# A circuit stage's first 20 microseconds in another order: Sin's table, the scans, sixteen columns, and who splits the weights

## The reference

```python
def quantum_circuit(v):
    return jnp.cumprod(jnp.cos(v), axis=-1)
x  = x + attention(layernorm(x), ctx, ctx)
xh = layernorm(x).reshape(B, T, H, dk)                 # 16 heads of 16 columns
x1 = layer_norm(xn + quantum_circuit(xh).reshape(B, T, C), gamma1, beta1)
q  = quantum_circuit(x1[..., :16])
h  = jnp.einsum('btq,fq->btf', q, w1) + b1             # 16 -> 1024
ffn = jnp.einsum('btf,cf->btc', jax.nn.relu(h), w2) + b2
x  = x + layer_norm(x1 + ffn, gamma2, beta2)
x  = x + experts(layernorm(x))
```

## Time and profile before

| | us |
| --- | --- |
| median of 3 runs (1952.27 to 1953.28) | 1952.32 |
| the profiled execution's own time | 1960.63 |
| its span in the profile | 1958.8 |
| TensorE busy in the span | 1885.8 |
| VectorE busy | 1468.4 |
| ScalarE busy | 1134.9 |
| GpSimd busy | 650.0 |

### The profile page before, as it was taken

How to read it: one execution, slowest core, us unless ns; L and a number is a source line. 1 busy time by engine, 2 the same in 40 slices (tenths; PEclk the granted TensorE clock), 3 DMA queues, 4 the chain that set the end, 5 groups by cost and what they waited for, 6 DMA issues and landing times. The chain is left out here.

```text
span 1958.8 us, 46585 instructions
## 1 busy us (share of the span) xinstructions
PE 1885.8 (96%) x18804; PEld 1783.4 (91%) x18804; DVE 1468.4 (75%) x2800; ACT 1134.9 (58%) x1917; POOL 650.0 (33%) x636
## 2 busy tenths in 40 slices
PE   7899999999999999999999999999879889999998
PEld 5899999999999999999999999999757789999998
DVE  6777777777777777777777777777777567666667
ACT  2556655666665566666656665666656435566652
POOL 3222233322223232222323222233021135888960
PEclk9999999999999999999999999999969699999999
DMA  8666667666666666666666666667311136666633
GB/s 270 172 155 160 172 156 179 158 163 154 160 170 159 173 160 164 152 162 168 162 160 172 164 155 160 166 166 182 106 59 44 54 113 210 210 220 223 226 115 135
DMA packets 146790, 313.85 MB, mean 160 GB/s; under 512 B 57888, under 2 KB 77216, under 8 KB 143120
## 3 DMA queue, kind: packets, MB, share of 16 engines
q1 hardware_dynamic: 140672, 295.03, 55.7%
q0 software_dynamic: 4752, 13.38, 2.3%
q10 hardware_dynamic: 1152, 2.47, 0.5%
HBM read 134.20 MB, written 18.35 MB: 78 GB/s over the span
## 5 line engine op out<-in xcount | busy, mean ns | idle before, releaser
L440 ACT COPY a_pT<-a_pst 128x512 f32<-128x512 f32 x768 | 421.7, 583 | 412.8 <-PE a_pst L936 412.8
L446 ACT ACTIVATE a_probs<-a_probs,a_nmax 128x1601 f32<-128x1601 f32 x256 | 418.7, 1636 | 142.0 <-DVE a_probs L608 141.9
L608 DVE TENSOR_SCALAR_CACHE_REDUCE a_probs<-a_pss 128x1608 f32<-128x1608 f32 x256 | 467.5, 1826 | 12.4 <-PE a_pss L925 10.8
L936 PE MATMUL a_pst<-a_id,a_probs 128*128 128x128 f32 (+1 forms) x3328 | 454.9, 275 | 11.4 <-ACT a_pT L440 9.0
L936 PEld LDWEIGHTS a_pst<-a_id,a_probs 128*128 128x128 f32 (+1 forms) x3328 | 384.9, 141 | 49.6 <-issue 21.4
L353 POOL TENSOR_TENSOR a_tick<-a_tick 128x1 f32<-128x1 f32 x62 | 12.0, 193 | 951.0 <-DMA a_raw<-in_ctxT 865.2
L626 DVE TENSOR_SCALAR a_khi<-a_psk,a_bk 128x402 fp32r<-128x402 f32 x250 | 158.6, 635 | 143.5 <-PE a_psk L890 141.3
L358 POOL TENSOR_TENSOR a_clo<-a_raw,a_chi 128x402 fp32r<-128x402 f32 x240 | 247.4, 1062 | 4.8
L925 PE MATMUL a_pss<-a_kst,a_bd 96*128 96x402 f32 x1024 | 240.7, 357 | 8.0 <-DVE a_v L633 5.8
L888 PE MATMUL a_pso<-a_whi,a_chi 128*128 128x256 f32 (+1 forms) x806 | 241.3, 299 | 0.0
L890 PE MATMUL a_pso<-a_whi,a_clo 128*128 128x256 f32 (+1 forms) x806 | 226.6, 281 | 0.0
(11 more groups left out here) (248 smaller groups left out, 3511.7 us busy)
## 6 DMA issues: line engine op xcount, KB each, us to landing
a_kst<-a_khi SPq DMA_DIRECT2D x1008, 100.5 KB, 2.6
a_kst<-a_klo SPq DMA_DIRECT2D x504, 100.5 KB, 2.6
a_raw<-in_ctxT SPq DMA_DIRECT2D x60, 804.0 KB, 5.6
f_gur<-in_wgu SPq DMA_DIRECT2D x24, 1408.0 KB, 6.2
f_dr<-in_wd SPq DMA_DIRECT2D x24, 768.0 KB, 4.7
a_bd<-q_scr SPq DMA_DIRECT2D x192, 32.0 KB, 2.0
e_big<-ys_scr SPq DMA_DIRECT2D x8, 512.0 KB, 6.7
a_pT<-in_ctxT SPq DMA_DIRECT2D x2, 1608.0 KB, 8.8
```

Of the source, the lines that this page charges most:

```text
L440: nc.scalar.copy(pT[:, p % HALF, 4 * i:4 * i + 4, :], ps_t[:, i % 2, :].rearrange("p (t q) -> p t q", q=P)).then_inc(t_copied_act, 1)
L446: nc.scalar.activation(pr, pr, ACT.Exp, bias=nmax[:, b, p:p + 1], scale=-1.0, accum_out=esum[:, b, p:p + 1]).then_inc(probs_ready, 1)
L608: nc.vector.tensor_scalar(probs[:, p % 2, :].rearrange("p (b k) -> p b k", b=QK), ps_s[:, :, 0:KQ], -SCALE, None, ALU.mult, ALU.min, accum ...
L936: mm = nc.tensor.transpose(ps_t[0:r, i % 2, (t % 4) * P:(t % 4 + 1) * P], probs[:, p % 2, t * P:t * P + r], a_id_sb[:])
```

## The change

- ScalarE: Sin's table is loaded before the last three copies (`table.0`), cos.0 and cos.1 come next, then two copies, cos.2, the third copy, cos.3. The lists now hold these copies, and TensorE's holds the last transposes, the weighing and the projection, in the order as before.
- VectorE: `scan` is a stage of its own, apart from `residual`. All four lists are in a new order.
- `centre_q` scales only the first 16 columns of groups 0 and 1; `centre1` scales the other 240 of these groups later, and q_angles.0 and .1 wait for `centre_q` alone.
- GpSimd zeroes `heads` in four instructions (two of them before the keys are stacked), zeroes the first column of each head in `c` and in `qc`, which VectorE did, and splits w1, which VectorE did, ahead of its list. centre1 of the groups that lie where w1 was loaded waits for this split, and so does each first `expand` of a group.

```diff
         DVE_ORDER = order(
-            "rows.0 ends.0 residual.0 norms.0 residual.1 scale1.0 last_rows.0 scale1.1 q_angles.0 affine.0 circuit.0 q_angles.1 affine.1 circuit.1 residual.2 "
-            "residual.3 scale1.2 residual.4 scale1.3 add.0 sums.0 scale1.4 q_angles.2 scale2.0 q_angles.3 circuit.2 q_angles.4 circuit.3 circuit.4 add.1 sums.1 "
-            "round.5 reduce.5 scale2.1 second.0 affine.2 residual.5 second.1 scale1.5 add.2 scale3.0 scale3.1 affine.3 affine.4 q_angles.5 affine.5 circuit.5 add.3 "
...
+            "rows.0 scan.0 residual.0 ends.0 scan.1 scale1.0 residual.1 q_angles.0 norms.0 circuit.0 scan.2 residual.2 last_rows.0 scale1.1 scale1.2 affine.0 "
+            "q_angles.1 scan.3 circuit.1 q_angles.2 scan.4 circuit.2 residual.3 residual.4 add.0 scale1.3 sums.0 scale1.4 round.5 reduce.5 q_angles.3 q_angles.4 "
+            "scan.5 circuit.3 residual.5 scale2.0 affine.1 affine.2 circuit.4 add.1 affine.3 affine.4 add.2 scale1.5 second.0 q_angles.5 sums.1 circuit.5 scale3.0 "
+            "affine.5 add.3 sums.2 scale2.1 second.1 scale2.2 add.4 scale3.1 second.2 add.5 sums.3 scale3.2 scale2.3 second.3 add.6 sums.4 scale3.3 scale2.4 "
...
-            "cos.0 cos.1 cos.2 cos.3 cos.4 centre1.0 centre1.1 q_cos.0 angle.5 q_cos.1 copy_q.0 relu.0 relu.1 relu.2 relu.3 relu.4 relu.5 relu.6 copy_q.1 relu.7 "
-            "relu.8 relu.9 relu.10 relu.11 relu.12 relu.13 relu.14 relu.15 centre1.2 centre1.3 centre1.4 q_cos.2 centre2.0 q_cos.3 q_cos.4 copy_q.2 relu.16 relu.17 "
-            "copy_q.3 relu.18 relu.19 relu.20 relu.21 relu.22 relu.23 relu.24 relu.25 cos.5 copy_q.4 centre2.1 relu.26 relu.27 centre1.5 centre3.0 centre3.1 "
...
+            "table.0 cos.0 cos.1 copies.0 cos.2 copies_end.0 cos.3 centre_q.0 centre1.0 cos.4 q_cos.0 copy_q.0 relu.0 relu.1 relu.2 relu.3 relu.4 relu.5 relu.6 "
+            "relu.7 centre_q.1 centre1.1 centre1.2 q_cos.1 angle.5 copy_q.1 q_cos.2 relu.8 relu.9 relu.10 relu.11 copy_q.2 relu.12 relu.13 relu.14 relu.15 relu.16 "
+            "relu.17 centre1.3 centre1.4 cos.5 q_cos.3 relu.18 relu.19 relu.20 relu.21 copy_q.3 relu.22 relu.23 relu.24 relu.25 q_cos.4 centre2.0 relu.26 relu.27 "
+            "relu.28 copy_q.4 centre1.5 q_cos.5 exp_table.0 centre3.0 relu.29 relu.30 relu.31 copy_q.5 relu.32 copy_x.0 centre2.1 centre2.2 centre3.1 relu.33 "
+            "relu.34 relu.35 relu.36 relu.37 relu.38 relu.39 relu.40 centre2.3 relu.41 relu.42 centre3.2 relu.43 relu.44 relu.45 relu.46 relu.47 centre3.3 "
...
         PE_ORDER = order(
-            "turn_q.0 expand.0 expand.1 expand.2 expand.3 expand.4 expand.5 expand.6 expand.7 turn_q.1 expand.8 expand.9 expand.10 expand.11 expand.12 expand.13 "
-            "expand.14 expand.15 contract.0 contract.1 turn_q.2 expand.16 expand.17 turn_q.3 expand.18 expand.19 turn_q.4 expand.20 expand.21 expand.22 expand.23 "
-            "expand.24 expand.25 contract.2 expand.26 expand.27 contract.3 expand.28 expand.29 turn_x.0 expand.30 expand.31 turn_q.5 expand.32 turn_x.1 contract.4 "
...
+            "turn_last.0 turn_end.0 weigh.0 project.0 turn_q.0 expand.0 expand.1 expand.2 expand.3 expand.4 expand.5 expand.6 expand.7 contract.0 turn_q.1 expand.8 "
+            "expand.9 expand.10 expand.11 turn_q.2 expand.12 expand.13 expand.14 expand.15 expand.16 expand.17 contract.1 expand.18 expand.19 expand.20 expand.21 "
+            "turn_q.3 expand.22 expand.23 expand.24 expand.25 contract.2 expand.26 expand.27 turn_q.4 expand.28 contract.3 expand.29 expand.30 turn_x.0 expand.31 "
+            "turn_q.5 expand.32 contract.4 contract.5 expand.33 expand.34 expand.35 expand.36 expand.37 expand.38 expand.39 expand.40 expand.41 expand.42 "
+            "contract.6 expand.43 expand.44 expand.45 expand.46 expand.47 logits.0 contract.7 turn_x.1 turn_x.2 logits.1 turn_x.3 logits.2 turn_x.4 logits.3 "
+            "turn_x.5 turn_x.6 logits.4 logits.5 logits.6 turn_x.7 logits.7 ")
...
+        Q_FIRST = 2
+        HEADS_ZERO, C_ZERO, W1_ZERO, QHEADS_ZERO, QC_ZERO, QT_ZERO = 4, 5, 6, 7, 8, 9
...
-            sp.wait_ge(heads_zeroed, 1)
+            sp.wait_ge(zeroed, HEADS_ZERO)
...
-            for m in range(NC):
-                for z in range(PIECES):
-                    pool.wait_ge(stacked[m][z], COPIES * B)
-            nc.gpsimd.memset(heads[:], 0.0).then_inc(heads_zeroed, 1)
+            for i in range(0, NT, 4):
+                if i == NT // 2:
+
+                    for m in range(NC):
+                        for z in range(PIECES):
+                            pool.wait_ge(stacked[m][z], COPIES * B)
+                nc.gpsimd.memset(heads[:, i:i + 4, :], 0.0).then_inc(zeroed, 1)
             pool.wait_ge(s_filled, PAIRS * B)
             pool.wait_ge(o_filled, 2 * (B - 1))
-            nc.gpsimd.memset(w1_sb[:].bitcast(F32), 0.0).then_inc(heads_zeroed, 1)
-            nc.gpsimd.memset(q_heads[:], 0.0).then_inc(heads_zeroed, 1)
-            nc.gpsimd.memset(qT[:].bitcast(F32), 0.0).then_inc(heads_zeroed, 1)
+            nc.gpsimd.memset(c[:].rearrange("p t (h d) -> p (t h) d", d=HD)[:, :, 0], 0.0).then_inc(zeroed, 1)
+            nc.gpsimd.memset(w1_sb[:].bitcast(F32), 0.0).then_inc(zeroed, 1)
+            nc.gpsimd.memset(q_heads[:], 0.0).then_inc(zeroed, 1)
+            nc.gpsimd.memset(qc[:, :, 0], 0.0).then_inc(zeroed, 1)
+            nc.gpsimd.memset(qT[:].bitcast(F32), 0.0).then_inc(zeroed, 1)
+            pool.wait_ge(loaded, 16 * 7)
+            pool.wait_ge(zeroed, W1_ZERO)
+            nc.gpsimd.tensor_copy(w1_sb[0:3 * HD, :], w1_raw).then_inc(w1_split, 1)
+            pool.wait_ge(w1_split, 1)
+            nc.gpsimd.tensor_tensor(out=w1_sb[2 * HD:3 * HD, :], in0=w1_raw[2 * HD:, :], in1=w1_sb[2 * HD:3 * HD, :].bitcast(F32), op=ALU.subtract).then_inc(w1_split, 1)
+            pool.wait_ge(w1_split, 2)
...
-            g = PAIRS * B - 1
             act.wait_ge(expo_set, 1)
             act.wait_ge(kv_filled, STEPS * B)
-            for i in range(3):
-                copy_tiles(g, PAIRS - 1, i)
-            nc.scalar.activation(first_sin[:], x1_ex[:, 0:1], ACT.Sin)
 
             def centre(g, n, out, src):
 
                 act.wait_ge(scale_set[n], g + 1)
+                if n == 1 and sum(GROUPS[g]) > NT // 2:
+
+                    act.wait_ge(w1_split, 2)
+                cols = slice(HD if n == 1 and g < Q_FIRST else 0, D)
                 for i in each(g):
-                    last = nc.scalar.activation(out[:, i, :], src[:, i, :], ACT.Identity, bias=shift[:, i:i + 1], scale=rstd[:, i:i + 1])
+                    last = nc.scalar.activation(out[:, i, cols], src[:, i, cols], ACT.Identity, bias=shift[:, i:i + 1], scale=rstd[:, i:i + 1])
                 last.then_inc(centred[n], 1)
 
             for stage, g in ACT_ORDER:
                 f = lambda z: flat(z, g)
-                if stage == "angle":
+                if stage == "table":
+                    nc.scalar.activation(first_sin[:], x1_ex[:, 0:1], ACT.Sin)
+                elif stage == "copies":
+                    for i in range(2):
+                        copy_tiles(PAIRS * B - 1, PAIRS - 1, i)
+                elif stage == "copies_end":
+                    copy_tiles(PAIRS * B - 1, PAIRS - 1, 2)
+                elif stage == "centre_q":
+                    act.wait_ge(scale_set[1], g + 1)
+                    for i in each(g):
+                        last = nc.scalar.activation(a[:, i, 0:HD], t[:, i, 0:HD], ACT.Identity, bias=shift[:, i:i + 1], scale=rstd[:, i:i + 1])
+                    last.then_inc(q_centred, 1)
+                elif stage == "angle":
                     angles(units_to(g) - 1)
                 elif stage == "cos":
 
                     act.wait_ge(reduced, units_to(g))
-                    act.wait_ge(heads_zeroed, 1)
+                    act.wait_ge(zeroed, C_ZERO)
...
-                    act.wait_ge(heads_zeroed, 3)
+                    act.wait_ge(zeroed, QC_ZERO)
...
-            ch(nc.vector.memset(c[:].rearrange("p t (h d) -> p (t h) d", d=HD)[:, :, 0], 0.0))
-            ch(nc.vector.memset(qc[:, :, 0], 0.0))
 
             for stage, g in DVE_ORDER:
                 f = lambda z: flat(z, g)
@@ -829,23 +855,24 @@
                     leave_turns(units_to(g) - 1)
                 elif stage == "rows":
                     dve.wait_ge(loaded, 16 * 7)
-                    dve.wait_ge(heads_zeroed, 2)
-                    ch(nc.vector.tensor_copy(w1_sb[0:3 * HD, :], w1_raw))
                     ch(nc.vector.tensor_tensor(ffn_row[:], row[:, B1, :], row[:, FB, :], ALU.add))
                     ch(nc.vector.tensor_scalar(q_row[:, 0, :], row[:, G1, 0:HD], 1.0 / (2.0 * np.pi), None, ALU.mult))
                     ch(nc.vector.tensor_scalar(q_row[:, 1, :], row[:, B1, 0:HD], 1.0 / (2.0 * np.pi), 0.25, ALU.mult, ALU.add))
                     ch.wait()
-                    nc.vector.tensor_tensor(w1_sb[2 * HD:3 * HD, :], w1_raw[2 * HD:, :], w1_sb[2 * HD:3 * HD, :].bitcast(F32), ALU.subtract).then_inc(w1_split, 1)
```

(51 more changed lines are left out.)

## The result

Seven runs of the changed kernel have a median of 1946.94 us (1944.6 to 1947.65), seven of the kernel before 1953.56 (1952.27 to 1962.32). The two medians are 6.6 us apart. The ratio worked out from all the runs is 0.9952, interval 0.9935 to 0.9969: 0.3 to 0.65% faster, about 6 to 13 us, where 3.0 were forecast. In a later job on one chip the same kernel gave 0.9966 (0.9954 to 0.9977), and four variants that turned out equal to it 0.9960 to 0.9962. So the gain is some 7 to 9 us: 0.9966 to 0.9952 of 1953.56 is 6.6 to 9.4.

What follows compares the result with a forecast made beforehand. The prediction saw a ScalarE-VectorE chain bounding work up to expand.0, then TensorE and its clock. 5.7 us gained at the front, less 2.55 for a climb and smaller later terms, gave -3.0: 1949.3 us, range 1945.9 to 1953.3.

Steps and rivals of the forecast that it cites:

- the second climb of the clock: TensorE's narrow expands between contract.0 and contract.1: clock falls and must rise again, giving back 2.55 us.
- the end of the walk: TensorE from contract.7 to the last logits: one more turn_x pair at a falling clock shrinks the 4.1 us lead to 3.1.
- GpSimd's split and power at no cost: GpSimd's w1 split, about 2.7 us, ends before pow1.0 needs GpSimd; pow1.0 taken as 0 late, at most 1.2 us.
- Rival A: Clock holds through the narrow expands before contract.1, no new climb: -5.55 us, 1946.8 us; chance 0.26.
- The front: Chain of ScalarE and VectorE from the last exponential to expand.0: 5.7 us gained, scan.0 starting 4.0 us earlier.
- Contract.6: TensorE's contraction late in the stage: starts at the slow clock before and after the change, 9.62 us against 7.07 at full clock.
- The table: Sin's table on ScalarE ahead of the last copies: earlier cosines let VectorE's scan.0 start 4.0 us sooner.
- Sixteen columns: ScalarE scales 16 columns first, ending at 1436.35, so q_angles.0 can follow at 1437.8; extra instructions cost about 0.4 us.
- last_rows.0 later: VectorE's last tile sums move from 1443.4 to about 1446.8, delaying loads and a store on SP: cost nothing.
- B: One further climb before contract.7, or pow1.0 late by 1.2 us and the tail losing 1.3: -0.5 us, 1951.8; chance 0.16.
- C: Contract.1, contract.2 and contract.7 all start at the slow clock, 7.65 us paid: +2.1 us, 1954.4; chance 0.10.
- D: Reorder before expand.0 does nothing because the weighing or the projection sets it; chance 0.02.

Runs made afterwards that it cites:

- its repetition: Unchanged kernel profiled again: the kernel before 1956.92 us (ratio 1.0012); the changed kernel 1947.89 us (0.9966).
- the four memsets: Kernel before with only heads zeroed in four instructions, two before the stacked keys: 1952.91 us against 1955.19, ratio 0.9988.
- the table alone: Kernel before with only ScalarE's Sin table and first cosines moved ahead of the copies: 1953.87 us against 1955.75, ratio 0.9986.
- the memset twice: Heads zeroed whole, two times in a row: on the kernel before 1953.32 us (0.9994), on the changed kernel 1945.48 us (0.9960).
- two with the whole memset: Changed kernel with heads zeroed by one instruction after the stacked keys, run in two jobs: 1946.76 us (0.9960) and 1947.08 us (0.9962).
- all columns: Changed kernel without centre_q, so centre1 of groups 0 and 1 scales all 256 columns at once: 1946.96 us, ratio 0.9960.
- the version in pieces: Changed kernel with GpSimd's split of w1 cut into four casts and four subtractions of 256 columns: 1945.41 us, ratio 0.9962.
- both on VectorE: Changed kernel with w1's cast and subtraction done by VectorE again, run in two jobs: 1944.94 us (0.9943) and 1943.08 us (0.9949).

## Why the prediction was wrong

The direction held, and 1946.94 lies in the range, but the gain is more than twice the 3.0 us of the forecast. **Two terms of the sum were mis-sized, and they are the steps that failed: the second climb of the clock, charged at 2.55 us, measured 1.0, and the end of the walk, charged at 1.0, measured -0.7.** Another 1.4 us lie ahead of the stage, where the forecast had nothing. A third step failed in kind, GpSimd's split and power at no cost, and it failed the other way: it made the front 1.6 us worse than forecast and hid part of the error.

Five profiles have the old order (before, its repetition, the four memsets, the table alone, the memset twice), six the new one with GpSimd's whole split (after, its repetition, two with the whole memset, all columns, the memset twice). Means of these, each a mean of single executions:

| step | forecast | measured, old to new |
| --- | --- | --- |
| expand.0 after the last exponential | -5.7 | 19.5 to 15.5: -4.1 |
| contract.0 and .1 together | +2.55 | 15.7 to 16.7: +1.0 |
| rest up to contract.7's start | -1.0 | -1.7 (contract.7 at 99.5 to 94.7) |
| contract.7's start to the last logit | +1.0 | 22.7 to 22.0: -0.7 |
| the stage | -3.1 | 122.2 to 116.7: -5.5 |
| the last exponential's place in the span | 0 | 1426.3 to 1425.0: -1.4 |

(The second line: 64 matmuls in a row 15.7 us; parted 9.4 and 7.7, less 0.35 by which the rows of two pieces overlap what follows. The prediction's 4.1 us at contract.7 are taken at its end; by its own starts, 1526.6 against 1530.43, it is 3.8, so the third and fourth lines would be -0.7 and +0.7. Two of its readings are a little off as well: the clock rose 5.3 us after contract.0's start, not 5.6, by the 0.78 of 1462 to 1464, and fell 3.5 us after contract.5's end, not 4.)

- **The new climb, mis-sized**: 2.55 charged, 1.0 measured. The 2.55 came from contract.6 before, which lay under the half clock for its first 5 us. In the profile after the fall came 5.5 us after contract.0's end rather than 4, just before contract.1, and the clock was back 3.4 us later (0.98, 0.50 and 0.66 in the three stretches above). Contract.1 lost 1.0 to 1.6 us in three of the six profiles, and in the other three it ran at 7.1 us, without any. Rival A, no new climb, had the right mechanism half the time. That its number, 1946.8, is almost the measured one is luck: the profile after did have the fall, and the errors of the other terms nearly cancel.
- **The end of the walk, mis-sized**. The tail was charged 1.0 for a further pair of transposes; it is 0.7 shorter. The rows suggest why, though no run tests it: the new order puts logits.0 ahead of contract.7 and the next ones between the transposes, where eight matmuls take 1.06 us. In the kernel before, four groups of logits came after the fall of the clock and took 6.83 us, in the changed one three, 5.12:

```profile
1543.34 6.83 PE L1130 MATMUL f_psl<-f_wr,f_xT 128*128 128x7 f32 x32
```

```profile
1525.73 1.06 PE L1162 MATMUL f_psl<-f_wr,f_xT 128*128 128x7 f32 x8 [0.24 <-ACT f_xT L625]
...
1530.93 5.12 PE L1162 MATMUL f_psl<-f_wr,f_xT 128*128 128x7 f32 x24
```

- The front, failed in kind. Scan.0 was forecast at +2.85 and came at +3.7 to +4.1; pow1.0's wait was taken as 0 and cost 0.63. Both are **GpSimd beside VectorE's instructions**. The prediction sized the subtraction rightly (2.7 against 2.67) and counted it against pow1.0's need only (that held: it ended 1425.5, the variance came at 1429.4), and never what it does to VectorE. For the split this is shown by the version in pieces and by both on VectorE: moving it there costs some 2 us by the medians. For pow1.0 it is read from the profiles: 0.72 or 0.73 us in all five of the old order, 1.57 to 1.88 in every one of the new, where it meets scan.1. The prediction had named that case at 0.5 to 1.2 us and took 0, because it expected pow1.0 to come before the scan; in the profile after it began only 0.14 us before.
- Contract.6, which the walk took as slow on both sides, is slow by chance in either kernel (7.1 to 9.6). It was slow in the profile that the walk used and not in the one after, so that pair of profiles shows 2.55 us that no change brought.
- The table: 3.2 us by experiment, 4.0 forecast as the shift of scan.0. Sixteen columns: nothing. last_rows.0 later: nothing, as forecast; cos.5 ran at 1463, the store that it waits for had landed some 10 us earlier.
- The baseline. The one profile of the walk was a long execution (1960.63 against medians of 1953 to 1957), with contract.6 at 9.6 and the clock down before the last exponential. The prediction carried the difference over as a constant, where it belongs to a spread of over 10 us in the kernel before and of some 5 in the changed one.

Rivals: A is partly right; B, C and D did not occur as a whole, though B's late pow1.0 came, at 0.63 instead of 1.2 us. Three things stay open: what shortened the tail, why the changed kernel spreads less, and whether the earlier last exponential (1.4 us in the mean, of places that run from 1422.6 to 1428.4 in the old order and from 1422.2 to 1429.8 in the new) is anything but chance.

## What to carry to other kernels

Work moved to an engine that "has time" still has to be priced by what it does to its neighbour's instructions: look for the rows in which the neighbour's same operation lasted longer, not only for who waits. A reordering of several engines' lists is one thing; undoing a single entry of it (here contract.0) can cost more than the whole gain. And take more than one profile of the kernel before, and the price of a clock's fall from more than one place, when a clock that comes and goes makes single executions differ by more than the change.
